# Reordering the attention inner work of a transformer layer: alternating scratch halves, an earlier rotary tail, a later bound broadcast, and exponentials that run one key block behind

## The reference

```
q = proj(Wq, bq); k = proj(Wk, bk); v = proj(Wv, bv)
q = _apply_rotary(q, cos, sin); k = _apply_rotary(k, cos, sin)
attn = softmax(einsum('bhqd,bhkd->bhqk', q, k) * scale)
out  = einsum('bhqk,bhkd->bhqd', attn, v)
x = layernorm(x + out @ Wo.T + bo)
x = layernorm(x + moe(x))       # 8 experts, top 2, silu
```

## Time and profile before

| what | us |
|---|---|
| median of 8 runs | 3051.9 (3043.43 to 3462.14) |
| the profiled execution | 3043.43 |
| its span on the slowest core (core 2) | 3041.9 |
| spans of the eight cores | 3032.0 to 3041.9 |
| PE busy / ACT busy / DVE busy | 2573.6 / 593.4 / 773.4 |

### The profile page before, as it was taken

The page is one execution under the profiler, slowest core; times in us unless marked ns, Lnnn a source line. Parts: engine busy times, 40 slices in busy tenths (PEclk is TensorE's granted clock), DMA queues, the critical chain, the costliest instruction groups (busy, mean ns, idle before and its releaser), DMA issues.

```text
span 3041.9 us, 31002 instructions; the slowest of 8 cores (3032.0 to 3041.9 us)
## 1 busy us (share of the span) xinstructions
PE 2573.6 (85%) x12053; PEld 1192.7 (39%) x12262; DVE 773.4 (25%) x1140; ACT 593.4 (20%) x761; POOL 172.3 (6%) x323
## 2 busy tenths in 40 slices
PE   4778788888887878799479998999999899998993
PEld 3234343435353525244134343444434344443441
DVE  0222222222212131321632213122221312212226
ACT  0332424242424333342100000000000000000031
POOL 1000000000000000000000001010000101001000
PEclk9889999999998989899589999999999999999996
DMA  9210101010101010024124344443434444344423
GB/s 154 43 28 15 28 15 28 14 28 15 28 14 28 15 28 8 7 36 76 26 51 77 63 76 64 69 76 64 78 59 77 70 69 76 63 76 63 70 45 121
DMA packets 50720, 155.26 MB, mean 51 GB/s; under 512 B 6162, under 2 KB 6290, under 8 KB 49298
## 3 DMA queue, kind: packets, MB, share of 16 engines
q0 software_dynamic: 47264, 142.69, 28.2%
q1 hardware_dynamic: 3314, 10.59, 1.0%
HBM read 287.54 MB, written 8.39 MB: 97 GB/s over the span
## 4 chain that ended last, share of the span: by engine, by line
PE 74%; DVE 9%; DMA 9%; issue 4%; ACT 3%; DVEq 0%; ACTq 0%; POOL 0%; POOLq 0%
PE pb L769 15%; PE pb L786 14%; PE pb L843 9%; DMA wslab<-w_t 6%; PE pb L318 6%; PE pb L395 6%; PE pb L389 5%; PE pb L441 4%; PE pb L462 4%; PE pb L532 4%; PE pb L448 4%; DMA R_bf<-x_t 2%; DVE scr_f L339 1%; ACT scr_bf L355 1%; PE pb L364 1%
## 5 line engine op out<-in xcount | busy, mean ns | idle before, releaser
L843 PE MATMUL pb<-aog,wslab 128*128 128x512 bf16 x2006 | 456.9, 380 | 58.2 <-DMA wslab<-w_t 55.5
L769 PE MATMUL pb<-xy,wslab 128*128 128x512 bf16 x2004 | 462.6, 387 | 3.4 <-issue 1.3
L786 PE MATMUL pb<-xy,wslab 128*128 128x512 bf16 x2011 | 450.5, 379 | 1.9
L780 ACT ACTIVATE scr_bf<-pb 128x512 bf16<-128x512 f32 x128 | 69.5, 594 | 1321.7 <-PE pb L769 1321.6
L843 PEld LDWEIGHTS pb<-aog,wslab 128*128 128x128 bf16 x2048 | 194.5, 98 | 316.9 <-issue 96.7
L469 ACT ACTIVATE scr_bf<-pb,mq_sb 128x1024 bf16<-128x1024 f32 x256 | 285.0, 1114 | 135.9 <-PE pb L462 135.7
L395 PE MATMUL pb<-R_bf,wslab 128*128 128x512 bf16 x768 | 297.6, 387 | 8.0 <-ACT vbuf L306 5.9
L769 PEld LDWEIGHTS pb<-xy,wslab 128*128 128x128 bf16 x2048 | 203.0, 100 | 253.0 <-issue 21.2
L786 PEld LDWEIGHTS pb<-xy,wslab 128*128 128x128 bf16 x2048 | 200.4, 98 | 241.7
L389 PE MATMUL pb<-R_bf,wslab 128*128 128x512 bf16 x728 | 283.0, 389 | 0.0
L856 DVE TENSOR_TENSOR R_f<-pb,R_f 128x512 f32<-128x512 f32 x256 | 177.1, 692 | 340.0 <-PE pb L843 326.7
(11 more groups left out here) (111 smaller groups left out, 1456.6 us busy)
## 6 DMA issues: line engine op xcount, KB each, us to landing
wslab<-w_t POOLq DMA_DIRECT2D x128, 512.0 KB, 5.1
wslab<-w_t POOLq DMA_DIRECT2D x128, 256.0 KB, 3.8
wslab<-wv_t POOLq DMA_DIRECT2D x8, 1024.0 KB, 8.4
R_bf<-x_t POOLq DMA_DIRECT2D x16, 512.0 KB, 7.1
wslab<-wq_t POOLq DMA_DIRECT2D x8, 1024.0 KB, 8.8
wslab<-wk_t POOLq DMA_DIRECT2D x8, 1024.0 KB, 8.3
wslab<-wo_t POOLq DMA_DIRECT2D x16, 512.0 KB, 5.1
y<-R_f SPq DMA_DIRECT2D x16, 512.0 KB, 2.6
```

Of the source, the lines that this page charges most:

```text
L769: last = t.matmul(pa[nc2].ap(), wslab.ap()[:, W1OFF[s1] + dc * 128: W1OFF[s1] + dc * 128 + 128], xy.ap()[:, dc * TL + nc2 * 512: dc * TL + ...
L786: last = t.matmul(pa[4 + nc2].ap(), wslab.ap()[:, W3OFF[s1] + dc * 128: W3OFF[s1] + dc * 128 + 128], xy.ap()[:, dc * TL + nc2 * 512: dc * ...
L843: last = t.matmul(pa[wb + nc2].ap(), wslab.ap()[:, W2OFF[s2] + fc * 128: W2OFF[s2] + fc * 128 + 128], aog.ap()[:, fc * TL + nc2 * 512: fc ...
```

## The change

Four edits, all inside a head.

1. `emit_evac_pair` and `emit_tail_pair` choose the half of `scr_bf` by the pair: the first pair of a projection keeps its copy in `sb2,sb3` and its squares in `sb0,sb1`, the second key pair does the opposite.
2. The tail of the first key pair is recorded behind the third of the sixteen steps of the second pair's projection, not behind the last.
3. The matmul and the negation that end the bound move out of `bound_finale` into a new function `bound_bcast`. It writes bank 6 in place of bank 3 and is recorded inside `st_merged`, behind the score matmuls of key blocks 0 and 1, so behind the second key pair's tail.
4. In `st_merged` the scores of blocks 0 and 1 come first; then, for each block from 2 on, its scores, the exponential of the block before it, and the sums and value products of the block two before it. The exponential of an even block now writes `sb2,sb3`, that of an odd block `sb0,sb1`.

No arithmetic is added or removed: the number of instructions per engine is the same.

```diff
 def emit_tail_pair(a):
+    qso = 1024 if (a // 2) % 2 == 0 else 0
+    qk = ["sb2", "sb3"] if qso else ["sb0", "sb1"]
     for q2 in range(2):
         T(... t.matmul(pa[2 + q2].ap(), ps_sb.ap(),
-            scr_bf.ap()[:, 1024 + q2 * 512: 1024 + q2 * 512 + 512], ...),
-            r=[f"sb{2 + q2}", "pswap"], w=[f"pa{2 + q2}"])
+            scr_bf.ap()[:, qso + q2 * 512: qso + q2 * 512 + 512], ...),
+            r=[qk[q2], "pswap"], w=[f"pa{2 + q2}"])
...
 def emit_evac_pair(a, pbt, pbkeys):
+    qso = 1024 if (a // 2) % 2 == 0 else 0
+    sqo = 1024 - qso
...
     for dc in range(NDC):
         T(pmm, r=[f"R1_{dc}"] + wkeys, w=[f"pa{pb[0]}", f"pa{pb[1]}"])
-    if pr >= 1:
-        emit_tail_pair(a - 2)
+        if dc == 2 and pr >= 1:
+            emit_tail_pair(a - 2)
     emit_evac_pair(a, pb_[pb[0] // 2], ...)
...
+def bound_bcast():
     T(lambda t: t.matmul(
-        pa[3].ap()[:, 0:1], ones_r_f.ap(), msc.ap()[0:1, 7:8],
-        start=True, stop=True), r=["msc", "ones"], w=["pa3"])
+        pa[6].ap()[:, 0:1], ones_r_f.ap(), msc.ap()[0:1, 7:8],
+        start=True, stop=True), r=["msc", "ones"], w=["pa6"])
     V(lambda v: v.tensor_scalar(
-        mq_sb.ap()[:, 6:7], pa[3].ap()[:, 0:1], -1.0, None, ...
+        mq_sb.ap()[:, 6:7], pa[6].ap()[:, 0:1], -1.0, None, ...
...
-def st_merged():
-    for kc in range(NDC):
-        ...          # scores of kc, exponential of kc
-        if kc >= 1:
-            sums_pvs(kc - 1)
-    sums_pvs(NDC - 1)
+def st_merged(pre=None):
+    emit_mms(0)
+    emit_mms(1)
+    if pre is not None:
+        pre()
+    emit_exp(0)
+    for kc in range(2, NDC):
+        emit_mms(kc)
+        emit_exp(kc - 1)
+        if kc >= 2:
+            sums_pvs(kc - 2)
+    emit_exp(NDC - 1)
+    sums_pvs(NDC - 2)
+    sums_pvs(NDC - 1)
...
-st_merged()
+st_merged(pre=bound_bcast)
```

More of the change, by code:

```diff
@@ L332, in emit_tail_pair @@
                 def emit_tail_pair(a):
+                    qso = 1024 if (a // 2) % 2 == 0 else 0
+                    qk = ["sb2", "sb3"] if qso else ["sb0", "sb1"]
                     for q2 in range(2):
-                        T(lambda t, a=a, q2=q2: t.matmul(
+                        T(lambda t, a=a, q2=q2, qso=qso: t.matmul(
                             pa[2 + q2].ap(), ps_sb.ap(),
-                            scr_bf.ap()[:, 1024 + q2 * 512: 1024 + q2 * 512 + 512],
+                            scr_bf.ap()[:, qso + q2 * 512: qso + q2 * 512 + 512],
                             start=True, stop=True),
-                            r=[f"sb{2 + q2}", "pswap"], w=[f"pa{2 + q2}"])
+                            r=[qk[q2], "pswap"], w=[f"pa{2 + q2}"])
                     V(lambda v, a=a, sin=sin: v.tensor_tensor(
@@ L342, in emit_tail_pair @@
                         r=["pa2", "pa3", "sk"], w=["sf0", "sf1"])
-                    V(lambda v, a=a, cos=cos: v.tensor_tensor(
-                        scr_f.ap()[:, 1024:2048], scr_bf.ap()[:, 1024:2048],
+                    V(lambda v, a=a, qso=qso, cos=cos: v.tensor_tensor(
+                        scr_f.ap()[:, 1024:2048], scr_bf.ap()[:, qso:qso + 1024],
                         cos.ap()[:, a * 512: a * 512 + 1024], ALU.mult),
-                        r=["sb2", "sb3", "ck"], w=["sf2", "sf3"])
+                        r=qk + ["ck"], w=["sf2", "sf3"])
                     V(lambda v, a=a: v.tensor_tensor(
@@ L354, in emit_evac_pair @@
                 def emit_evac_pair(a, pbt, pbkeys):
-                    A(lambda s, pbt=pbt: s.activation(
-                        scr_bf.ap()[:, 1024:2048], pbt.ap(), AF.Identity,
-                        bias=bcol.ap()[:, hh:hh + 1]),
[L358 to L362, removed]
+                    qso = 1024 if (a // 2) % 2 == 0 else 0
+                    sqo = 1024 - qso
+                    qk = ["sb2", "sb3"] if qso else ["sb0", "sb1"]
+                    sk_ = ["sb2", "sb3"] if sqo else ["sb0", "sb1"]
+                    A(lambda s, pbt=pbt, qso=qso: s.activation(
+                        scr_bf.ap()[:, qso:qso + 1024], pbt.ap(), AF.Identity,
+                        bias=bcol.ap()[:, hh:hh + 1]),
+                        r=pbkeys + [bckey], w=qk)
+                    V(lambda v, qso=qso, sqo=sqo: v.tensor_tensor(
+                        scr_bf.ap()[:, sqo:sqo + 1024], scr_bf.ap()[:, qso:qso + 1024],
+                        scr_bf.ap()[:, qso:qso + 1024], ALU.mult),
+                        r=qk, w=sk_)
                     for q2 in range(2):
-                        T(lambda t, q2=q2: t.matmul(
+                        T(lambda t, q2=q2, sqo=sqo: t.matmul(
                             pa[4 + q2].ap(), ones_sq.ap(),
-                            scr_bf.ap()[:, q2 * 512: q2 * 512 + 512],
+                            scr_bf.ap()[:, sqo + q2 * 512: sqo + q2 * 512 + 512],
                             start=True, stop=True),
-                            r=[f"sb{q2}", "ones"], w=[f"pa{4 + q2}"])
+                            r=[sk_[q2], "ones"], w=[f"pa{4 + q2}"])
                     if nt == 2:
@@ L435, in emit_group, with emit_mms @@
                       [f"kb{hl}_{i}" for i in range(4)], finale=bound_finale)
-            def st_merged():
[L438 to L456, removed]
-                for kc in range(NDC):
+            def st_merged(pre=None):
+                def emit_mms(kc):
                     j = kc % 2
@@ L468, in st_merged, with emit_exp @@
                             w=[f"pa{2 * j + qb}"])
-                    A(lambda s, j=j: s.activation(
-                        scr_bf.ap()[:, j * 1024:(j + 1) * 1024],
+                def emit_exp(kc):
+                    j = kc % 2
+                    so = (1 - j) * 1024
+                    A(lambda s, j=j, so=so: s.activation(
+                        scr_bf.ap()[:, so:so + 1024],
                         pb[j].ap(), AF.Exp, bias=mq_sb.ap()[:, 6:7],
@@ L473, in st_merged, with sums_pvs @@
                         r=[f"pa{2 * j}", f"pa{2 * j + 1}", "mq"],
-                        w=[f"sb{2 * j}", f"sb{2 * j + 1}"])
-                    if kc >= 1:
-                        sums_pvs(kc - 1)
+                        w=[f"sb{2 * (1 - j)}", f"sb{2 * (1 - j) + 1}"])
+                def sums_pvs(kc):
+                    j = kc % 2
+                    so = (1 - j) * 1024
+                    for qb in range(2):
+                        T(lambda t, kc=kc, so=so, j=j, qb=qb: t.matmul(
+                            pa[6 + qb].ap(), ones_sq.ap(),
+                            scr_bf.ap()[:, so + qb * 512: so + qb * 512 + 512],
+                            start=(kc == 0), stop=(kc == NDC - 1),
+                            skip_group_check=True),
+                            r=[f"sb{2 * (1 - j) + qb}", "ones"], w=[f"pa{6 + qb}"])
+                        T(lambda t, kc=kc, so=so, j=j, qb=qb, hl=hl: t.matmul(
+                            pa[4 + qb].ap(),
+                            vbuf.ap()[:, kc * 256 + hl * 128:
+                                      kc * 256 + hl * 128 + 128],
+                            scr_bf.ap()[:, so + qb * 512: so + qb * 512 + 512],
+                            start=(kc == 0), stop=(kc == NDC - 1),
+                            skip_group_check=True),
+                            r=[f"sb{2 * (1 - j) + qb}", f"vb{kc}"],
+                            w=[f"pa{4 + qb}"])
+                emit_mms(0)
[10 more added lines that the diff above has]
+                sums_pvs(NDC - 2)
                 sums_pvs(NDC - 1)
```

4 lines of the change are left out of this document (2 added, 2 removed).

## The result

The changed kernel takes 3024.4 us (median of 11 runs, lowest 3011.28) against 3052.3 before; the ratio is 0.9895, with a 95% interval of 0.9882 to 0.9907, so 28 to 36 us less. The medians hold some executions in which one die ran at a lower clock, and the ratio leaves those out. The profiled executions took 3043.43 and 3014.48 us: 29 us less where 19 were forecast. The attention ends earlier by 34 us (its last value product ends at 1288.1 us in place of 1321.9); on the core that is slowest now, the later stages took 5 us more than on the one that was slowest before.

A forecast was written before the change was run, and what follows sets the result against it. PE sets the end, stalling ahead of the sums of squares (146.0 us) and for the bound (40.9 us), with half-clock stretches. -15 and -4 make -19 us on 3043.4: 3024 us (3033 on the median base), range 3008 to 3052.

The forecast's parts named there:

- Early tail: First key pair's tail runs during the second pair's projection; the stall behind the second copy shrinks 2.43 us, -38.9 us over sixteen heads.
- Late bound: Bound behind the second key pair's tail: 2.56 us wait per head goes, two waits replace it, first exponential at 8.4 us.
- Sine wait: Before the second block's scores, PE waits for the tail's sine product: 2.4 us a head instead of 0.63.
- second idle span: Before the third block's scores, PE waits for the first exponential, from about 6.8 to 9.65 us after the copy: 2.9 us.
- Loop: Loop over key blocks in the new order: still 2.86 us for two blocks, gain 0; bounds 0 to -31 us.
- The rival that the loop speeds up: In the key-block loop, scores two blocks ahead let PE run at its own pace: -31 us more, 2993 us; 7 in 100.
- Long half-clock stretch: At each head's loop start, half clock ends 14.2 us after the second key copy; net -0.93 us a head, -15 in all.
- the sixth exponential: Point in each head's loop from which both kernels run alike; forecast 17.7 us after the second key copy, against 16.2 before.
- The rival without a half clock: At each loop's start, shorter stalls keep the clock up: -3.2 us a head, -52 us, 2992 us; 7 in 100.
- the slower one with a longer stretch: At each loop's start, half clock lasts to 17.6 us: +0.5 us a head, +8 us, 3051 us; 16 in 100.
- Short stretches: The 13 to 15 half-clock stretches of 3.4 us following some stalls: a few fewer, -4 us; bounds -22 to +22.
- by more than a handful: Sign of being wrong: the number of short half-clock stretches, 13 to 15 before, changes by more than a handful.

The follow-up runs named there:

- the kernel with the bound back: Changed kernel with the bound's matmul and negation returned to the end of `bound_finale`, ahead of the second key pair's tail: 0.9874 of before, profiled 3012.38 us.
- 16 extra matmuls: Changed kernel plus 16 unused matmuls in the middle of each first key pair's projection, 3.45 us a head: 1.0072 of before, profiled 3070.88 us.
- shifting one stall by 1.72 us: Changed kernel plus 8 unused matmuls in the middle of each first key pair's projection: 1.0065 of before, profiled 3066.64 us.
- the deferred version: Kernel with the negation ahead of the cosine product, plus query's and first key pair's squares and tails behind the next projection's sixth step: 0.9483, profiled 2892.39 us.
- the old loop: Changed kernel with `st_merged` in its old order, the bound still behind the tail: 0.9884 of before, profiled 3015.01 us.

## Why the prediction was right, and where it was off

- **Early tail.** The stall went from 4.69 to 2.21 us (forecast 2.26), the key copies from 12.62 to 10.14 us apart (10.19). The run with the early tail alone shows that nothing else of the change is needed for it, the alternating halves included.
- **Late bound.** Sine wait 2.29 us (2.4), second idle span 2.83 (2.9), first exponential 8.27 after the copy (8.4). The mechanism, a negation queued on DVE behind three long operations, is in the rows, and moving it with the scores and the matmul ahead of it brought the first exponential from 8.27 to 5.91 us and saved 33 us.
- **Loop.** No gain (0), 2.86 us for two blocks in both orders. The rival that the loop speeds up is gone.
- **Long half-clock stretch.** It ended about 14.5 us after the copy (14.2), and the sixth exponential came at 17.75 (17.7). So the -15 us of this part were nearly right: (17.75 - 16.2) - (12.62 - 10.14) = -0.93 a head, and summed over the sixteen heads of both traces -13 us. The end at 14.2 was chosen past the 13.8 that the rows gave, because PE has less to do just before; no run tested that reason, and that the choice fits is in part luck. The rival without a half clock and the slower one with a longer stretch did not come. Where gaps of 2.29 and 2.83 us follow each other the clock fell to 0.50 in every head. The rule in the Trainium skill, "TensorE: Matmul & The Clock Gate", section "Why this matters for your kernels", which names longer gaps only, does not describe this kernel.
- **Short stretches: the step that was off.** The prediction wrote "I expect a few fewer" and "take -4 us". All thirteen went: over the sixteen heads the way from the query's copy to the first key copy got 10.0 us shorter, the one between the key copies 3.2 more than the stall explains, and the one between the groups 8.8, together -22 us, the end of the bounds that it had given. A change "by more than a handful" was a sign of being wrong that it had set itself, and it came. The ground that it named, three stalls at equal distances, does not hold. The early tail alone and the kernel with the bound back have the same distances (10.14 to 10.19 us where no short stretch lies in them) and keep sixteen and fifteen; 16 extra matmuls make them 13.65 and 10.14, and none comes back. What the runs show in its place: the short ones are gone where the tail is early and the bound late, and not with one of the two; and shifting one stall by 1.72 us brings sixteen back, by 3.46 none. What makes one place good and another bad stays open.

-13 and -22 make -35. The attention's last value product comes 34 us earlier; its first head starts 1.7 us later, and the rest of the heads differs by 0.6. That the time fell into the range is owed to the range's width, not to an understanding of the short stretches.

## What to carry to other kernels

Count what is queued on each engine behind an instruction that moves, and follow the wait to the engine that sets the end: here that gave the first exponential to 0.13 us. A stall of PE that waits for two other engines is best filled with the next matmuls at hand, as the deferred version does. Where the clock falls near stalls, two kernels with different waits can take the same time, so a change is judged by its rows and not by the total alone.

## What had not been expected of the hardware

Four kernels with quite different waits (the change, the early tail alone, the bound back, the old loop) take the same time within 3 us, 3012.4 to 3015.2, and in each of them a group of two heads takes 153.6 to 153.8 us, the mean of the first seven groups from query copy to query copy. With 8 and with 16 extra matmuls in the middle it is 160.7 and 160.5 us. What one wait gained came back, wholly or in part, as time at half clock elsewhere: 26 of 29 us with the bound back, 32 of 63 with the negation ahead of the cosine product. That the clock's changes hold the heads in step is argued from these equal times and from the stretches that start at the same place in head after head; it was not shown by itself, and the kernel before, with 158.0 us a group and stretches at changing places, does not show it.
